# State-space scan and attention with mixture of experts on one core: the last batch's tail moved into the second block, the last norm moved to ScalarE, dt rebuilt

## The reference

```
x = L0_attn_x                                        # 8 x 512 x 128
x = x + layernorm(ssm(layernorm(x)))                 # "x1" below is this sum
x = x + layernorm(attn_moe(layernorm(x)))

def ssm(x):                                          # two directions, f and b (b on the flipped sequence)
    xn = layernorm(x) * norm_g + norm_b
    u, z = split(xn @ Win.T); u = silu(conv1d(u, 4 taps) + convb)
    dtr, B, C = split(u @ Wx.T, [8, 24])
    dt = softplus(dtr @ Wdt.T + bdt)                 # 512 x 256
    h_t = exp(dt_t * A) * h_(t-1) + (dt_t * u_t) * B_t   # 256 channels x 16 states, along 512 tokens
    y = (h . C + u * D) * silu(z);  return y @ Wout.T    # result: x + y_f + y_b

def attn_moe(x):     # RMS norm, q k v, rotation, causal attention (16 heads of 8, 4 kv heads), then
    ...              # RMS norm, top 2 of 8 experts, each silu(h w1) * (h w3) @ w2, weighted sum
```

## Time and profile before

| what | value |
|---|---|
| median of 3 runs | 1732.66 us (1731.58 to 1736.15) |
| the profiled execution's own time | 1733.05 us |
| its span in the profile | 1731.3 us |
| mean granted PE clock | 0.891 |
| busy: PE, DVE, ACT, POOL | 77%, 80%, 61%, 64% |

### The profile page before, as it was taken

The page is one execution under the profiler, slowest core; times in us unless marked ns, Lnnn a source line. Parts: engine busy times, 40 slices in busy tenths (PEclk is TensorE's granted clock), DMA queues, the critical chain, the costliest instruction groups (busy, mean ns, idle before and its releaser), DMA issues. The chain is left out here.

```text
span 1731.3 us, 30902 instructions
## 1 busy us (share of the span) xinstructions
PE 1340.6 (77%) x8880; PEld 970.1 (56%) x8880; DVE 1387.3 (80%) x2234; ACT 1063.0 (61%) x1888; POOL 1109.6 (64%) x1244
## 2 busy tenths in 40 slices
PE   4878787778778787877787647798988889888671
PEld 2656566556656665656566423345665566556561
DVE  2999999999999999999999645676878777776422
ACT  6777676786776777767767215565655565546230
POOL 2777777787778777878777624454646666545435
PEclk8898899899899898998898768888999999999886
DMA  5112302320222023113203021134645545563672
GB/s 191 60 46 99 123 4 94 122 98 18 104 98 116 7 98 122 52 46 122 98 19 120 24 91 43 43 119 153 193 139 180 172 136 173 171 191 120 207 213 71
DMA packets 115418, 186.12 MB, mean 108 GB/s; under 512 B 10752, under 2 KB 87680, under 8 KB 111104
## 3 DMA queue, kind: packets, MB, share of 16 engines
q1 hardware_dynamic: 111200, 176.36, 29.6%
q0 software_dynamic: 4096, 8.40, 1.7%
HBM read 153.99 MB, written 26.15 MB: 104 GB/s over the span
## 5 line engine op out<-in xcount | busy, mean ns | idle before, releaser
L1021 POOL TENSOR_TENSOR hc<-hb,cb 128x512 f32<-128x512 f32 x512 | 653.9, 1296 | 199.1 <-DVE hb L873 168.9
L873 DVE TENSOR_TENSOR_SCAN hb<-da,dbu 128x512 f32<-128x512 f32 x448 | 527.7, 1205 | 16.8 <-PE dbu L440 8.7
L711 ACT ACTIVATE da<-dt,a_neg 128x512 f32<-128x512 f32 x512 | 351.5, 716 | 184.3 <-DVE hb L873 157.3
L477 PE MATMUL yp<-ident,hc 128*128 128x128 f32 x2048 | 322.6, 292 | 5.7 <-POOL hc L1021 5.3
L1967 ACT ACTIVATE pt<-scores,lift 128x512 f32<-128x512 f32 x320 | 216.3, 683 | 172.9 <-PE scores L1712 165.4
L477 PEld LDWEIGHTS yp<-ident,hc 128*128 128x128 f32 x2048 | 272.9, 153 | 87.0 <-issue 54.3
L2097 DVE TENSOR_REDUCE mx<-ms 128x1 f32<-128x384 f32 (+3 forms) x352 | 218.2, 636 | 103.7 <-PE ms L1674 96.6
L857 DVE TENSOR_TENSOR dbu<-dtu,bp 128x512 f32<-128x512 f32 x384 | 251.2, 684 | 14.1 <-PE bp L465 4.3
L2438 POOL TENSOR_SCALAR_AFFINE_SELECT pt<-pt 128x256 f32<-128x256 f32 (+1 forms) x320 | 118.2, 372 | 201.5 <-ACT pt L1967 199.6
L388 PE MATMUL wp<-xpad,wu 128*128 128x512 f32 x256 | 131.8, 606 | 11.6 <-DVE res L888 6.5
L1674 PE MATMUL ms<-k,q 72*128 72x384 bf16 (+3 forms) x512 | 137.2, 326 | 0.0
(11 more groups left out here) (251 smaller groups left out, 2398.5 us busy)
## 6 DMA issues: line engine op xcount, KB each, us to landing
cb<-c_scratch SPq DMA_DIRECT2D x16, 3072.0 KB, 11.7
wt<-ffn_w_e SPq DMA_DIRECT2D x120, 384.0 KB, 4.4
cb<-c_scratch SPq DMA_DIRECT2D x16, 1024.0 KB, 4.6
q<-q_scratch SPq DMA_DIRECT2D x96, 96.0 KB
xg<-xs_scratch SPq DMA_DIRECT2D x24, 256.0 KB, 3.4
ys_scratch<-ysb SPq DMA_DIRECT2D x24, 256.0 KB
q_scratch<-qp SPq DMA_DIRECT2D x21, 128.0 KB
k<-k_scratch SPq DMA_DIRECT2D x32, 72.0 KB
```

The lines of the kernel that those rows point to most:

```text
L477: last = nc.tensor.matmul(yp[:, c, h * P:(h + 1) * P], src[:, c * P:(c + 1) * P], ident[:, :], is_transpose=True, start=(s < 0 and h == 0 ...
L711: nc.scalar.activation(da[:, s % NDA, :], dt[:, h, :], ACT.Exp, scale=a_neg[:, d, h, n:n + 1]).then_inc(da_done, 1)
L873: nc.vector.tensor_tensor_scan(hb[:, s % NHB, :], da[:, s % NDA, :], src, 0.0, ALU.mult, ALU.add).then_inc(scan_done, 1)
L1021: nc.gpsimd.tensor_tensor(hc[:, s % NHC, :], hb[:, s % NHB, :], cb[:, d, s // 2, :], ALU.mult).then_inc(hc_done, 1)
```

## The change

Three things are changed.

1. The way between the blocks. `ident`, the weight tiles `wt`, the q and k tiles and two PSUM tensors (`yp`, `wp`) are allocated once and used by both blocks, under other names. Small tiles of the first block (`hb`, `sz`, `res`, `x1t` and others) now lie in `wt`, and direction 0's C rows in the memory of q and k (a view shows them as `wt` and `qk`). The tail of the last batch is no longer at the end of the first block: its functions are handed to the second block, which calls them at the start (PE, ACT, and DVE's `yg`) and at slots -30, -24, -22 and -16. The loads of q and k for batch 0 are issued at the end of the first block. The `FIRST_...` steps in unit (7, 1) stand four to six slots earlier.
2. dt. The bias comes in by a row of ones in the matmul, the relu on ACT is gone, and DVE makes dt in two halves, max(PSUM, 0) + ln, as the siblings at slots 28 and 29, in place of one addition of 1024 columns at slot 29. `bt` and the first diagonals move from behind slot 31 of ACT to slot 1 of the next unit, and PE's transposes of B now wait for dt.
3. The last norm of the state-space batch. ACT makes `x1t` at its slot 24, in four activations with scale and bias, in place of DVE at slot 18. POOL computes the bias in two more small instructions, and its addition of the input moves from slot 18 to slot 24.

The diff, cut to its core:

```diff
-FIRST_IN = (8, 9)
+FIRST_IN = (2, 4)
...
-FIRST_POOL = (25, 29, 30, STEPS)
+FIRST_POOL = (19, 23, 24, 28)
+FIRST_ONES = 8
...
-DIAG_AT = ((-1, 5, 18, 20), (-1, 5, 11, 20))
+DIAG_AT = ((1, 5, 18, 20), (1, 5, 11, 20))
...
             sp_first_store(sp)
-            sp_store(sp, NB - 1)
             sp.wait_ge(first_stored, 16 * 8)
-            sp.wait_ge(x1_stored, count(x1_stored, NB - 1, 16))
+            sp.wait_ge(hc_done, count(hc_done, NB - 1, STEPS))
+            for g in range(NKV):
+                qk_in(sp, q9, k9, ffn["q"], ffn["k"], g, g, first_loaded[g], first_ones)
...
         def pe_bt(pe, b, d):
-            pe.wait_ge(soft_done, count(soft_done, b, 8 * d + 8))
+            pe.wait_ge(dt_done, count(dt_done, b, 3 * d + 2))
+            pe.wait_ge(soft_done, count(soft_done, b, 6 * d + 6))
...
             pe_unit(pe, NB - 1, 1, tail=(NB - 1, 0))
-            pe_ygt(pe, NB - 1, 1, last_unit=True)
-            for c in range(TC):
-                pe_out(pe, NB - 1, c)
...
-            elif k == 1:
-                nc.scalar.activation(t_relu[:, h, :], wp[:, 1 - (h ^ d), :], ACT.Relu, bias=bias).then_inc(soft_done, 1)
...
+        def act_x1(act, b):
+            act.wait_ge(end_rstd, count(end_rstd, b, 4))
+            act.wait_ge(x1_stored, count(x1_stored, b, 0))
+            for c in range(TC):
+                nc.scalar.activation(x1t[:, c, :], res[:, c, :], ACT.Identity, bias=rstd[:, 3, c:c + 1],
+                                     scale=rstd[:, 1, c:c + 1]).then_inc(x1_norm, 1)
...
                 if tail and s in (14, 15):
                     act_ygt(act, *tail, s - 14)
+                if tail and tail[1] == 1 and s == 24:
+                    act_x1(act, tail[0])
...
-                nc.vector.tensor_tensor(dt[:, :, :], t_ln[:, :, :], t_relu[:, :, :], ALU.add).then_inc(dt_done, 1)
+                nc.vector.scalar_tensor_tensor(dt[:, k, :], wp[:, 1 - (k ^ d), :], 0.0, t_ln[:, k, :],
+                                               ALU.max, ALU.add).then_inc(dt_done, 1)
...
-                        i = nc.vector.tensor_scalar(x1t[:, c, :], res[:, c, :], mv[:, 1, c, 0:1],
-                                                    rstd[:, 1, c:c + 1], ALU.subtract, ALU.mult)
...
-                if front and s in (29, 30):
-                    dve_dt(dve, *front, s - 29)
+                if front and s in (28, 29, 30):
+                    dve_dt(dve, *front, s - 28)
...
+            nc.gpsimd.tensor_scalar(rstd[:, 2, :], mv[:, 1, :, 0], -1.0, None, ALU.mult).then_inc(end_rstd, 1)
...
+            nc.gpsimd.tensor_tensor(rstd[:, 3, :], rstd[:, 2, :], rstd[:, 1, :], ALU.mult).then_inc(end_rstd, 1)
...
-                if tail and tail[1] == 1 and s == 18:
+                if tail and tail[1] == 1 and s == 24:
                     pool_x1(pool, tail[0])
...
+            if t % MAX_GROUP == 0 and is_first(b):
+                pe.wait_ge(ending["qk_loaded"][t // MAX_GROUP], 64)
...
                 if f == 0 and i == 0:
                     pe.wait_ge(casts, 2)
+                    ending["pe_wait_res"](pe)
...
+            ending["dve"](dve, -1)
             for s in slots():
```

More of the change, by code:

```diff
@@ L130, in sig, with part @@
             return s
-        ident = sb("ident", [P, P])
-        win_u = sb("win_u", [P, NDIR, DI])
+        NDA, NHB, NHC = 8, 4, 8
+        ident, yp, wp = shared["ident"], shared["yp"], shared["wp"]
+        taken = 0
+        def part(*shape):
+            nonlocal taken
+            names = " ".join("abcd"[:len(shape)])
+            n = int(np.prod(shape))
+            a = shared["wt"][:, taken:taken + n]
+            taken += n
+            return a.rearrange(f"p ({names}) -> p {names}", **dict(zip("abcd", shape)))
+        sz = part(NDIR, TC, DI)
+        yg = part(TC, DI)
+        ygt = part(NDIR, NH2, SEQ)
+        wout = part(NDIR, NH2, DM)
+        xres = part(2, TC, DM)
+        res = part(TC, DM)
+        x1t = part(TC, DM)
+        hb = part(NHB, SEQ)
+        dtt = part(TC, DI)
+        stats = part(2, TC, 6)
+        mv = part(2, TC, 2)
+        rstd = part(4, TC)
+        mhalf = part(2, TC)
+        eps = shared["wt"][:, taken:taken + TC]
+        q9, k9 = shared["q9"], shared["k9"]
         win_z = sb("win_z", [P, NDIR, DI])
@@ L741, in act_front @@
                 for h in range(NH2):
-                    for k in range(4):
+                    for k in range(3):
                         act_soft(act, b, d, h, k)
@@ L969, in _ @@
             dve_unit(dve, NB - 1, 1, tail=(NB - 1, 0))
-            dve_yg(dve, NB - 1, 1)
-            for k in range(4):
-                if k == 2:
-                    dve.wait_ge(end_step, count(end_step, NB - 1, 4))
-                dve_end(dve, NB - 1, k)
         def pool_ln_rstd(pool, b):
@@ L1083, in _, with pe_last, pe_wait_res, act_last @@
             pool_first(pool, STEPS)
-            pool_end_rstd(pool, NB - 1)
-            pool_x1(pool, NB - 1)
+        def pe_last(pe):
+            pe_ygt(pe, NB - 1, 1, last_unit=True)
+            for c in range(TC):
+                pe_out(pe, NB - 1, c)
+        def pe_wait_res(pe):
+            pe.wait_ge(res_done, count(res_done, NB - 1, 1))
+        def act_last(act):
+            act_ygt(act, NB - 1, 1, 0)
+            act_ygt(act, NB - 1, 1, 1)
+        def dve_last(dve, k):
+            if k < 0:
+                dve_yg(dve, NB - 1, 1)
+            else:
+                if k == 2:
+                    dve.wait_ge(end_step, count(end_step, NB - 1, 4))
+                    dve.wait_ge(end_rstd, count(end_rstd, NB - 1, 0))
+                dve_end(dve, NB - 1, k)
+        def pool_last(pool, k):
+            if k == 0:
+                pool_end_rstd(pool, NB - 1)
+            else:
+                pool_x1(pool, NB - 1)
+        def sp_last(sp):
+            sp_store(sp, NB - 1)
+        def sp_last_stored(sp):
+            sp.wait_ge(x1_stored, count(x1_stored, NB - 1, 16))
+        def act_last_x1(act):
+            act_x1(act, NB - 1)
+    return {"act_x1": act_last_x1, "pe": pe_last, "pe_wait_res": pe_wait_res, "act": act_last, "dve": dve_last, "pool": pool_last,
+            "sp": sp_last, "sp_stored": sp_last_stored, "qk_loaded": first_loaded}
 NHEAD, NKV, HD = 16, 4, 8
@@ L1180, in last_plan, with qk_in @@
     return {}
-MADE_BEFORE = ("xa", "in", "in_rstd", "norm", "h0", "ht", "ht_copy", "rope", "qk_add", "part", "qk_part", "parts_out")
+MADE_BEFORE = ("xa", "in", "in_rstd", "norm", "h0", "ht", "ht_copy", "rope", "qk_add", "part", "qk_part", "parts_out", "parts_in")
+LAST_X1 = -22
+def qk_in(sp, q9, k9, qscr, kscr, g, at, done, ones=None):
+    for a in range(3):
+        sp.dma_start(q9[a * 3 * HD:(a + 1) * 3 * HD, at].rearrange("r h s -> r (h s)"),
+                     qscr[a:a + 1, :, GH * g:GH * (g + 1)].rearrange("a d h s -> a d (h s)")
+                     .to_broadcast([3, HD, GH * SEQ])).then_inc(done, 16)
+    if ones is not None:
+        sp.wait_ge(ones, 1)
+    sp.dma_start(k9[0:PART_ROWS, at:at + 1].rearrange("r h s -> r (h s)"),
+                 kscr[:, :, g:g + 1].rearrange("b d h s -> b d (h s)").rearrange("b d n -> (b d) n")
+                 .unsqueeze(0).to_broadcast([3, 3 * HD, SEQ])).then_inc(done, 16)
 def due_table():
@@ L1897, in _ @@
                 pe.sem_inc(s, already)
+            ending["pe"](pe)
             for s in slots():
@@ L2055, in _ @@
                 act.sem_inc(s, already)
+            ending["act"](act)
             for s in slots():
@@ L2309, in dve_slot @@
                     dve_moe(dve, f, k)
+            if s == -30:
+                for k in range(3):
+                    ending["dve"](dve, k)
             for f, i in max_at(b, t):
@@ L2463, in pool_slot @@
             b, t = s // ST_TILES, s % ST_TILES
+            if s == -30:
+                ending["pool"](pool, 0)
+            if s == LAST_X1:
+                ending["pool"](pool, 1)
             for f, k in due("qk_add", s):
```

207 lines of the change are left out of this document (99 added, 108 removed).

## The result

The changed kernel takes 1742.28 us in the median of 9 runs (1734.2 to 1751.02), the kernel before, run beside it, 1731.58 (1724.29 to 1737.51): ratio 1.007, 95% interval 1.0037 to 1.0103. On another chip it was 1.012 (1.0063 to 1.0177). It is slower. The profiled execution took 1746.72 us, its span is 1745.0.

What follows compares the result with a forecast made beforehand. DVE was taken to bound the first block. From the profiled 1733.05 us, +27.9 for the norm, -11 for dt, -1.3 for relus and -10 for the way gave 1738.5 us; own range 1733 to 1745, over all 1706 to 1750.

Steps and rivals of the forecast that it cites:

- The place of the norm: Units (b+1, 0): x1t on ACT delays silu and PE's z by 2.4 us, so DVE waits at scan 25; +27.9 us.
- what the lower clock costs: Units (b+1, 0): all seven go like slow unit (7, 0), 18.86 + 2.4 = 21.2 us from scan 16 to 25.
- The default of the halved clock: PE ahead of z: by the skill's rule, the wait of 5.2 us gives the slow case in each unit.
- SPq held by the late addition: SPq at the unit's end: POOL's later addition delays C rows and next input some 4 us; taken as 0.
- rival C: Units (b, 1), slot 1: DVE waits 1 to 2 us for late input; 1746 to 1752; with another rival 0.15.
- dt: DVE's dt: two halves take about 1.3 us instead of 2.05, saved fifteen times; -11 us.
- the relus: ACT in the first unit, where DVE waits for ln: two relus of 0.67 us fewer; -1.3 us.
- The way: Between the blocks: the second block starts at 994 to 997 instead of 1005.0 on the old scale; -10 us.
- the meeting: Between the blocks: SPq's sixteen q and k loads, 12 to 14.5 us, now set when the engines meet.

Runs made afterwards that it cites:

- e1: Changed kernel with x1t back on DVE and POOL's addition back at slot 18 in the seven looped units: 1711.98 us, 0.994 of the kernel before.
- e6: Changed kernel with only group 0's four q and k loads issued at the first block's end, the other twelve in the second block: 1.007 of the kernel before.
- e11: Kernel before with one edit, ACT's silus of every unit at slot 24 in place of 25: 0.995 of the kernel before.
- e2: Changed kernel with direction 1's C rows ahead of the x1 store and the xres refills on SPq: 1.012 of the kernel before.
- e10: Changed kernel with x1t between the silus at slot 24, POOL's addition at 28, C rows first, only group 0's loads early: 1706.74 us, 0.983 of the kernel before.

## Why the prediction was right, point by point

**The place of the norm** was right in mechanism and sign: ACT's order, the table load +2.4 (measured +2.47), PE's idle 5.2 (5.64), `z` at the lower level in all seven units. The size was off: +27.9 forecast, +19.7 measured. The mis-sized term is what the lower clock costs. I carried the whole of unit (7, 0), 2.9 us of slowness, into each unit; measured are 20.05 - 15.96 - 2.47 = 1.6 us. In unit (2, 0) only the first four `z` matmuls took 2.07 us, the second four 1.37, and everything behind them ran at full speed. The longer wait does bring the lower level in every unit, but half of the slow stretch now passes while PE is idle (3.4 us), where in (7, 0) only 0.7 us of it did. The default of the halved clock held, as the Trainium skill says in "TensorE: Matmul & The Clock Gate", Part 1.

**SPq held by the late addition** was rival C, and half right: the C rows do leave late, but the input's landing cost nothing (DVE never waits for it in units (b, 1)). The cost is at the loop's end, 17.3 us, through DVE's own instructions. I had put this term at 0, and no step of mine had the instruction queue in it.

**dt**: the duration was right, 0.684 us a half, and DVE's work at dt fell from 31.9 to 21.9 us. The step that failed is the one that booked all of it as time, 11 us and 1.3 for the relus. In the changed kernel 7.9 of these 12.3 us are left. Where the norm is not late nothing is: e1 has dt and its six pairs take 710.8 us against 710.0. DVE works 5.2 us less there (8.5 less at dt, but 3.5 more at x1t, whose instructions take 543 ns each in place of 397) and waits 6.0 us more, at slots 9, 16 and 25. I asked of each part only whether it shortens DVE's row, not which new waits it puts into it.

**The way**: -10 forecast, -9.0 measured. SPq's loads set the meeting, as said (12.4 us behind scan 31; I said 14). The scores came 14.1 us behind the block's start, not 11.5, because `ht` landed behind the sixteen loads (9.7 us; in e6, where it stands ahead of twelve of them, the scores come 11.6 us behind the start). e1, which has the way and dt without the norm, is 9.5 us faster than before, and its first scores come 9.2 us sooner behind scan 31: the way's size.

**The rest**, -6.4 us behind the first scores, can't be told from nothing. The second block's code is the same in the kernel before and in e11, and from the first scores it took 714.6 and 725.2 us; the changed kernel's two profiles have 708.2 and 716.2. PE has the same 4398 instructions there in e2 and in e10, and (length, busy, clock)

```profile
1024.70:1729.20 704.50, 561.98 (x4398) 0.91 0.47 147
```

```profile
972.10:1707.80 735.70, 594.80 (x4398) 0.86 0.45 142
```

31 us apart, the longer one at the lower mean clock. In single profiles only the first block can be compared to a few us.

**The sum.** The profile's span grew by 13.7 us where the terms gave 5.6. The difference of 8.1 is 17.3 left out at the loop's ends, 4.4 too much for dt, 1.0 too much for the way, less 8.2 too much for the norm and the 6.4 of the rest. That 1738.5 stands so near to 1742.28 is in part luck: errors larger than the forecast's whole sum cancelled.
